# Four chained cross-attentions on one core: second layer through its values in fp32, epsilon on ScalarE, two layer norms centred in the weights, a new order of steps

## The reference, cut to what matters

```python
x = x + softmax(Q K^T / 16) V Wo + bo            # L0: Q from x, K and V from ctx
# L1: two attentions on layer norms, then a layer norm and a dense layer
x1n = ln(x) * g1 + b1 ; x2n = ln(ctx or side) * g2 + b2
x = x + attn_a(x1n, ctx_n) + attn_v(x1n, side_n)
x = x + ln(x) * g + b @ fc_W + fc_b
# L2: softmax over the queries (axis 1), not the keys; then a layer norm
w = softmax((x Wq + bq)(ctx Wk + bk)^T / 16, axis=1)
x = ln(w (ctx Wv + bv) + x) * gamma + beta
x = x + softmax(Q K^T / 16) V Wo + bo            # L3: like L0
```

## Time and profile before

| | value |
|---|---|
| profiled execution | 647.02 us, span 645.1 us |
| median of three runs | 645.7 us |
| TensorE matmul (PE) | 590.6 us busy, 4852 instructions |
| TensorE weight load (PEld) | 569.8 us, 4852 |
| VectorE (DVE) | 558.3 us, 1690 |
| GpSimd (POOL) | 524.4 us, 699 |
| ScalarE (ACT) | 434.4 us, 1462 |
| DMA | 43.97 MB, mean 68 GB/s |
| mean granted TensorE clock | 0.988 |

### The profile page before, as it was taken

One profiled execution on the slowest core, in us unless ns is written; L12 is line 12 of the kernel. 1 busy time (PEld: TensorE's weight loads), 2 busy tenths in 40 slices (PEclk: granted clock), 3 DMA queues, 4 the chain that ended last, 5 costly groups with the idle time before them and its releaser, 6 DMA issues. The chain is left out here.

```text
span 645.1 us, 16889 instructions
## 1 busy us (share of the span) xinstructions
PE 590.6 (92%) x4852; PEld 569.8 (88%) x4852; DVE 558.3 (87%) x1690; ACT 434.4 (67%) x1462; POOL 524.4 (81%) x699
## 2 busy tenths in 40 slices
PE   5987999998789988998998999999999999999976
PEld 4977998898789988988998999898999889999975
DVE  0687799999898989899879898989998998997993
ACT  1568867775658776666767768766668668767543
POOL 5489999997779988888888699888889898876772
PEclk8999999999999999998999999999999999999998
DMA  8931110031121221111212112113022000000011
GB/s 243 359 127 65 52 50 34 26 123 59 50 74 60 74 69 49 59 65 44 86 64 66 43 59 91 58 58 108 10 77 97 27 25 18 1 19 17 18 50 50
DMA packets 29514, 43.97 MB, mean 68 GB/s; under 512 B 2672, under 2 KB 21232, under 8 KB 29424
## 3 DMA queue, kind: packets, MB, share of 16 engines
q1 hardware_dynamic: 29424, 42.89, 20.2%
HBM read 34.49 MB, written 8.39 MB: 66 GB/s over the span
## 5 line engine op out<-in xcount | busy, mean ns | idle before, releaser
L900 ACT ACTIVATE prob_L<-bank,neg_max_L 128x128 f32<-128x128 f32 x320 | 114.4, 374 | 78.8 <-DVE neg_max_L L1168 77.5
L1316 POOL TENSOR_SCALAR xhat_ln<-x,rstd_ln,shift_ln 128x256 f32<-128x256 f32 x128 | 72.2, 573 | 20.4 <-issue 10.1
L1034 DVE TENSOR_TENSOR oT_lo_L<-bank,oT_hi_L 128x256 fp32r<-128x256 f32 (+1 forms) x128 | 60.9, 480 | 18.7 <-ACT oT_hi_L L843 18.0
L1310 POOL TENSOR_TENSOR rstd_ln<-var_eps_ln,minus_half 128x2 f32<-128x2 f32 x64 | 45.5, 711 | 31.5 <-DVE var_eps_ln L1135 28.5
L843 ACT ACTIVATE oT_hi_L<-bank 128x256 fp32r<-128x256 f32 (+1 forms) x128 | 57.1, 451 | 20.0 <-PE bank L666 18.9
L843 ACT ACTIVATE xT_hi_L<-bank 128x512 fp32r<-128x512 f32 (+1 forms) x96 | 58.1, 613 | 17.7 <-PE bank L636 15.9
L900 ACT ACTIVATION_READ_ACCUMULATOR prob_L<-bank,neg_max_L 128x1 f32 x320 | 67.4, 211 | 0.0
L1168 DVE TENSOR_REDUCE neg_max_L<-bank 128x2 f32<-128x256 f32 (+1 forms) x128 | 59.8, 479 | 3.0 <-PE bank L660 2.1
L843 ACT ACTIVATE probT_L<-bank 128x256 f32<-128x256 f32 (+1 forms) x96 | 44.2, 467 | 23.1 <-PE bank L644 23.0
L653 PE MATMUL bank<-xT_hi_L,M_hi_L 128*128 128x256 f32 x128 | 40.5, 316 | 9.6 <-DVE xT_lo_L L1034 5.4
L644 PE MATMUL bank<-ident,prob_L 128*128 128x128 f32 x256 | 44.1, 276 | 5.5 <-ACT prob_L L900 4.2
(11 more groups left out here) (208 smaller groups left out, 2400.3 us busy)
## 6 DMA issues: line engine op xcount, KB each, us to landing
x_in<-in_x SPq DMA_DIRECT2D x32, 512.0 KB, 3.5
ctx_in<-in_ctx SPq DMA_DIRECT2D x32, 256.0 KB, 2.7
out<-y SPq DMA_DIRECT2D x32, 256.0 KB, 2.2
side_in<-in_side SPq DMA_DIRECT2D x32, 128.0 KB, 2.1
WqT_L<-in_L_WqT SPq DMA_DIRECT2D x3, 256.0 KB, 4.0
Wo_L<-in_L_Wo SPq DMA_DIRECT2D x2, 256.0 KB, 4.3
WkT_L<-in_L_WkT SPq DMA_DIRECT2D x3, 128.0 KB, 5.3
WvT_L<-in_L_WvT SPq DMA_DIRECT2D x2, 128.0 KB, 3.6
```

The costliest lines, as they stand in the source:

```text
L900: last = activation(at(prob[k], g)[:, b, :], block(bank, b), ACT.Exp, bias=at(neg_max[k], g)[:, b:b + 1], accum_out=at(total[k], g)[:, b:b ...
L1034: dve.tensor_tensor(to, of, hi.bitcast(F32), ALU.subtract).then_inc(done[step], 1)
L1310: pool.tensor_tensor(at(rstd[k], g)[:], at(var_eps[k], g)[:], minus_half[:, 0:n], ALU.pow).then_inc(done[f"rstd_{k}"], 1)
L1316: last = pool.tensor_scalar(at(to, g)[:, n, :], tile, at(rstd[k], g)[:, n:n + 1], at(shift[k], g)[:, n:n + 1], ALU.mult, ALU.add)
```

## The change

- **Second layer.** O_L2, its sums, oT_hi_L2, oT_lo_L2, sums_L2 and x3_bias go. A new step V_L2 on TensorE multiplies the hi and lo parts of ctx^T by Wv (six fp32r matmuls of 256 columns) and v_L2 on VectorE adds the bias row while it evicts. OUT_L2 then is one plain fp32 product of 256 columns per sample, probabilities times values, and out_L2 adds x3 itself. hi_ctx and lo_ctx also wait until V_L2 has read their buffers.
- **Epsilon.** The four additions per group become activations on ScalarE (Identity with epsilon as bias column), between VectorE's mean and GpSimd's rstd.
- **Centring.** keys and ln1 are no longer shifted: GpSimd multiplies by rstd alone. The mean is taken out of WqT, WkT and WvT of L1a and L1v on VectorE at the start, after gains have been multiplied into them (WqT on VectorE, the others on GpSimd) from broadcast rows; new columns bqp and bvp carry the norm's biases. M0 and N0 of L1 go. M and N of L1 no longer need scale columns.
- **Loads.** Rows for g1, b1, g2 and b2 of both attentions (each 256 wide for L1's x side, 128 wide for the keys) replace the two gains; fewer columns in `cols`. L3's weights use L0's buffers and their loads wait for L0's products M, m, N and n.
- **Order.** All due times in STARTS (now of 94 steps) and PREPARATIONS are new, for example M_L1a from 1027 to 1381, M_L1v from 1116 to 2081, N_lo_L1v from 1478 to 2929, m_col_L3 from 2352 to 3377; V_L2 stands straight behind B2 in most groups. Rings: V2 three buffers, x3_bias and token_sums gone, the others unchanged.

```diff
+            def load_qk_L3():
+                prepared(sp, "M_L0")
+                prepared(sp, "m_L0")
+                two("L3", "WqT", "WkT", "qk")
+
+            def load_vo_L3():
+                prepared(sp, "N_L0")
+                prepared(sp, "n_L0")
+                two("L3", "WvT", "Wo", "vo")
+
...
+            def load_rows_wq(a):
+                def of():
+                    replicated(rows[f"{a}_b1"], f"{a}_b1", f"rows_wq_{a}")
+                    replicated(rows[f"{a}_g1"], f"{a}_g1", f"rows_wq_{a}")
+                return of
+
+            def load_rows_wkv(a):
+                def of():
+                    replicated(rows[f"{a}_g2"], f"{a}_g2", f"rows_wk_{a}")
+                    replicated(rows[f"{a}_b2"], f"{a}_b2", f"rows_wv_{a}")
+                return of
 
...
-            def O_L2(g):
+            def V_L2(g):
+
+                if g == 0:
+                    prepared(pe, "Wv2_lo")
+                pe.wait_ge(done["lo_ctx"], g + 1)
+                bank = bank_for(pe, "V_L2", g)
+                hi, lo = at(ctxT_hi, g), at(ctxT_lo, g)
+                for b in range(GROUP):
+                    to = bank[:, b * D:(b + 1) * D]
+                    mm(to, block(hi, b), Wv2_hi[:], start=True, stop=False)
+                    mm(to, block(hi, b), Wv2_lo[:], start=False, stop=False)
+                    last = mm(to, block(lo, b), Wv2_hi[:], start=False, stop=True)
+                last.then_inc(done["V_L2"], 1)
+
+            def OUT_L2(g):
+                pe.wait_ge(done["v_L2"], g + 1)
                 pe.wait_ge(done["prob_L2"], g + 1)
-                bank = bank_for(pe, "O_L2", g)
-                p = at(prob["L2"], g)
+                bank = bank_for(pe, "OUT_L2", g)
                 for b in range(GROUP):
-                    mm(block(bank, b), at(ctx_in, g)[:, b, :], p[:, b, :], start=True, stop=True)
-                for b in range(GROUP):
-                    last = mm(bank[:, TOK + b:TOK + b + 1], p[:, b, :], ones_col[:], start=True, stop=True)
-                last.then_inc(done["O_L2"], 1)
-
-            def OUT_L2(g):
-                if g == 0:
-                    prepared(pe, "Wv2_lo")
-                pe.wait_ge(done["oT_lo_L2"], g + 1)
-                projected("L2", g, [(Wv2_hi, Wv2_lo)])
+                    last = mm(bank[:, b * D:(b + 1) * D], at(prob["L2"], g)[:, b, :], at(V2, g)[:, b, :], start=True, stop=True)
+                last.then_inc(done["OUT_L2"], 1)
 
...
+            def eps_of(k, eps):
+                def of(g):
+                    if g == 0:
+                        prepared(act, "constants")
+                    act.wait_ge(done[f"mean_{k}"], g + 1)
+                    earlier(act, f"rstd_{k}", g, len(var_eps[k]))
+                    activation(at(var_eps[k], g)[:], at(mean_var[k], g)[:, :, 1], ACT.Identity,
+                               bias=epsilon[eps][:, 0:1]).then_inc(done[f"eps_{k}"], 1)
+                return of
...
-            def sums_L2(g):
-                act.wait_ge(done["O_L2"], g + 1)
-                earlier(act, "x3_bias", g, len(token_sums))
-                copied(at(token_sums, g)[:], bank_of("O_L2", g)[:, TOK:TOK + GROUP], "sums_L2")
-
...
+            def centred(w, sums_of, wait):
+
+                n = w.shape[2]
+                dve.tensor_reduce(sums_of[:], w[:], AX.X, ALU.add, negate=True).then_inc(done["small"], 1)
+                dve.wait_ge(done["small"], wait + 1)
+                dve.tensor_scalar(sums_of[:], sums_of[:], 1.0 / n, None, ALU.mult).then_inc(done["small"], 1)
+                dve.wait_ge(done["small"], wait + 2)
+                for t in range(T):
+                    last = dve.tensor_scalar(w[:, t, :], w[:, t, :], sums_of[:, t:t + 1], None, ALU.add)
+                return last
+
+            small = {}
+
+            def smalls(n):
+
+                small["raised"] = small.get("raised", 0) + n
+                return small["raised"] - n
+
+            def wq_of(a):
+                def of():
+                    w, product_of, b1 = stage[a]["WqT"], product["wq"], sums[f"b1_{a}"]
+                    dve.wait_ge(weights[f"{a}_qk"], TWO)
+                    dve.wait_ge(weights[f"rows_wq_{a}"], TWO)
+                    dve.wait_ge(weights["cols"], ONE)
+                    before = smalls(6)
+                    dve.tensor_tensor(product_of[:], w[:], rows[f"{a}_b1"][:].unsqueeze(1).to_broadcast([P, T, D]), ALU.mult).then_inc(done["small"], 1)
+                    dve.wait_ge(done["small"], before + 1)
+                    dve.tensor_reduce(b1[:], product_of[:], AX.X, ALU.add).then_inc(done["small"], 1)
+                    dve.wait_ge(done["small"], before + 2)
+                    dve.tensor_tensor(b1[:], b1[:], cols[:, COLS.index(f"{a}_bq"), :], ALU.add).then_inc(done["small"], 1)
+                    dve.wait_ge(done["small"], before + 3)
+                    dve.tensor_scalar(bqp[a][:].rearrange("p t o -> p (t o)"), b1[:], SCALE, None, ALU.mult)
+                    dve.tensor_tensor(w[:], w[:], rows[f"{a}_g1"][:].unsqueeze(1).to_broadcast([P, T, D]), ALU.mult).then_inc(done["small"], 1)
+                    dve.wait_ge(done["small"], before + 4)
+                    centred(w, sums[f"wq_{a}"], before + 4).then_inc(done[f"wq_{a}"], 1)
+                return of
+
...
+            def bvp_of(a):
+                def of():
+                    prepared(dve, f"wv_gained_{a}")
+                    dve.wait_ge(weights["cols"], ONE)
+                    before = smalls(1)
+                    b2 = sums[f"b2_{a}"]
+                    dve.tensor_reduce(b2[:], product["wv"][:], AX.X, ALU.add).then_inc(done["small"], 1)
+                    dve.wait_ge(done["small"], before + 1)
+                    dve.tensor_tensor(bvp[a][:].rearrange("p t o -> p (t o)"), b2[:], cols[:, COLS.index(f"{a}_bv"), :],
+                                      ALU.add).then_inc(done[f"bvp_{a}"], 1)
+                return of
+
...
-            def moments(k, g, tiles, eps, mean_used_by):
+            def moments(k, g, tiles):
 
                 st, mv = at(stats[k], g), at(mean_var[k], g)
                 for n, tile in enumerate(tiles):
                     last = dve.bn_stats(st[:, n, :], tile)
                 last.then_inc(done[f"stats_{k}"], 1)
                 dve.wait_ge(done[f"stats_{k}"], g + 1)
-                if mean_used_by:
-                    earlier(dve, mean_used_by, g, len(mean_var[k]))
+                earlier(dve, f"eps_{k}", g, len(mean_var[k]))
                 for n in range(len(tiles)):
                     last = dve.bn_aggr(mv[:, n, :], st[:, n, :])
                 last.then_inc(done[f"mean_{k}"], 1)
-                dve.wait_ge(done[f"mean_{k}"], g + 1)
-                earlier(dve, f"rstd_{k}", g, len(var_eps[k]))
-                if g == 0:
-                    prepared(dve, "constants")
-                dve.tensor_tensor(at(var_eps[k], g)[:], mv[:, :, 1], epsilon[eps][:, 0:len(tiles)], ALU.add).then_inc(done[f"var_{k}"], 1)
 
             def stats_keys(g):
                 dve.wait_ge(at(landed["ctx"], g), times_landed("ctx", g))
                 dve.wait_ge(at(landed["side"], g), times_landed("side", g))
                 tiles = [at(ctx_in, g)[:, b, :] for b in range(GROUP)] + [at(side_in, g)[:, b, :] for b in range(GROUP)]
-                moments("keys", g, tiles, EPS_L1, "shift_keys")
+                moments("keys", g, tiles)
 
...
-            def shift_of(k):
-                def of(g):
-                    dve.wait_ge(done[f"rstd_{k}"], g + 1)
-                    earlier(dve, f"norm_{k}", g, len(shift[k]))
-                    dve.scalar_tensor_tensor(out=at(shift[k], g)[:], in0=at(mean_var[k], g)[:, :, 0], scalar=-1.0,
-                                             in1=at(rstd[k], g)[:], op0=ALU.mult, op1=ALU.mult).then_inc(done[f"shift_{k}"], 1)
-                return of
+                moments("ln2", g, [at(x4, g)[:, b, :] for b in range(GROUP)])
+
+            def shift_ln2(g):
+                dve.wait_ge(done["rstd_ln2"], g + 1)
+                earlier(dve, "norm_ln2", g, len(shift["ln2"]))
+                dve.scalar_tensor_tensor(out=at(shift["ln2"], g)[:], in0=at(mean_var["ln2"], g)[:, :, 0], scalar=-1.0,
+                                         in1=at(rstd["ln2"], g)[:], op0=ALU.mult, op1=ALU.mult).then_inc(done["shift_ln2"], 1)
...
-            def x3_bias_of(g):
+            def v_L2(g):
                 if g == 0:
                     dve.wait_ge(weights["row_L2"], ONE)
+                dve.wait_ge(done["V_L2"], g + 1)
+                earlier(dve, "OUT_L2", g, len(V2))
+                dve.tensor_tensor(at(V2, g)[:], bank_of("V_L2", g)[:].rearrange("p (b d) -> p b d", d=D), every(bias["L2v"]),
+                                  ALU.add).then_inc(done["v_L2"], 1)
+
+            def out_L2(g):
                 dve.wait_ge(done["out_fc"], g + 1)
-                dve.wait_ge(done["sums_L2"], g + 1)
-                for b in range(GROUP):
```

(25 more changed lines are left out.)

260 lines of the change are left out of this document (135 added, 125 removed), and 358 rows, old and new, of tables (COPIES, EMPTIED_BY, PREPARATIONS, STARTS).

## The result

The changed kernel takes 601.2 us (median of 4 runs, 600.2 to 601.7) against 646.0 (644.9 to 648.2) for the kernel before on the same chip: a ratio of 0.930 with a 95% interval of 0.927 to 0.933. The forecast was 610 in a range of 594 to 636. The profiled execution took 600.2 us with a span of 598.1; its mean granted clock was 0.985 (0.988 before).

The account below looks back on a forecast made before the run. VectorE's SBUF-only instructions, held up by GpSimd, were taken to starve PE, which lost 50 us in the middle. 647.0 − 35 (middle) − 6 (ends) + 3.2 (second layer) + 2 (preparations) = 611, median 610 us; range 594 to 622, high end 636.

Parts of the forecast that it names:

- Rival (c): Nothing changes, since PE is full already (449 of 480 us busy): 651 us, or 646 to 649; chance 0.06.
- The −35: Middle, 80 to 560 us: at the 3.4% loss of its best comparable stretches, 430 us of work takes 445 us.
- That is about one for one: In two 50 us stretches, VectorE held up 7.1 and 3.0 us while PE lost 8.3 and 2.8.
- T: Theory on trial: VectorE instructions that stand still while GpSimd works empty TensorE, one for one.
- Epsilon's hold-up: VectorE's epsilon additions, all tensors in SBUF, stand still until GpSimd's running instruction is over: 43.0 us of 76 held up.
- I charge no PE time: Epsilon's 128 activations on ScalarE, 0.18 us each, 23 us (23 to 53), are hidden in its 142 us free.
- Rival (b): ScalarE's queue: eps steps wait for a mean and hold exps; 0.35 us each on PE's path gives 655 us; chance 0.08.
- GpSimd's norms: Norms of keys and ln1 with a constant in place of a shift column: GpSimd saves 0.45 us a group.
- Rival (a): GpSimd is next to bound: if it cannot exceed 86%, −14 us in the middle, 631 us; chance 0.20.
- The fp32 product: OUT_L2 on PE: two products of two instructions, 4 x 0.222 = 0.89 us a group; net +3.2 us with the second layer's trades.
- Preparations: VectorE's centring of L1a and L1v weights at the start: some 14 us, 25 us slack as cover, taken +2 us.
- near 440 to 455: VectorE's busy time in us after the change, from 558 to about 438 plus preparations.

Follow-up runs that it names:

- f: All of the change in the kernel before's order (its due times for shared steps), with eight V2 buffers: 616.5 us, ratio 0.957.
- g: Kernel before with the new second layer alone (V_L2, fp32 OUT_L2, v_L2), old order, eight V2 buffers: 640.0 us, ratio 0.994.
- l: g with epsilon and all shifts on VectorE in 128x1 pieces, old order: 631.2 us, ratio 0.980.
- n: g with epsilon on ScalarE, shifts and norms as before: three executions at 625.2 to 626.2 us, one at 615.7; median 625.6, no ratio formed.
- h: g with epsilon added as a constant and the shifts in 128x1 pieces: 643.5 us, ratio 0.999.
- b: Changed kernel with epsilon back on VectorE as a tensor_scalar with a constant (one SBUF input): 617.3 us, ratio 0.958.
- a: Changed kernel with epsilon's four additions back on VectorE as a tensor_tensor of two SBUF tiles: 618.5 us, ratio 0.960.
- j: a with epsilon on VectorE in single 128x1 columns, ten instructions a group: 612.1 us, ratio 0.950.
- m: Changed kernel with GpSimd's norms of keys and first layer norm adding a column of zeros in place of multiplying by a constant: 607.6 us, ratio 0.942.
- e: Kernel before with epsilon added as a constant by tensor_scalar and the shifts in 128x1 pieces: 643.2 us, ratio 0.997.
- i: Changed kernel with the last shift (second layer's norm) as two 128x1 tensor_scalars: 601.0 us, ratio 0.934.

## Why the prediction was right, and where not

**The outcome.** The direction and the range held; the forecast was 36 us of gain, and 45 came. By the sum's own terms: the middle gave 44 us for 35; the two ends 4.6 (42.9 lost to 38.3, by the earlier trace rows and the table), preparations included, for 6 less 2; the work grew from 552.2 to 554.1 us by the ruler, 1.9 for 3.2 (twelve small matmuls went, and the ruler has the forecast's price of the fp32 product in it). The reading that PE's busy time overstates it and that it lost 50 us carried the forecast, and it held: pace in the middle 8.4 matmuls per us (forecast about 8.5), 7.9 before. Rival (c), that PE was full, fell with it. The −35 was not made with the one-for-one rate: it took the whole middle to the pace of its best stretches. That the total came so near is in part luck. The stretches were picked for their small hold-up, which was one price among several; f, which lacks only the order, gives 36.4 in the middle and loses 3.8 more at the ends, and the order, priced at nothing, brought the rest. The forecast thus lies between two kernels that it did not tell apart: f (616.5 us) would have been 6 above the forecast, after is 9 below it.

**The step that failed** is "That is about one for one", the price of a stalled VectorE microsecond. Two stretches in which hold-up and loss happened to agree were read as a rate. Over eight stretches of 50 us of the kernel before (100 to 300, 350 to 400, 450 to 600) the three lines were held up for 52 us and TensorE lost 38; from 500 to 550 it was 8.7 for 4.5. The runs show this in its place, in the middle and in the old order:

| kernel | hold-up | VectorE busy | TensorE loses |
|---|---|---|---|
| before | 62 | 439 | 50 |
| g | 49 | 417 | 40 |
| l | 0 | 419 | 32 |
| n | 30 | 395 | 27 |
| f | 6 | 379 | 14 |

Where the hold-up went and nothing took its place on VectorE (before, g, n, f), 57 us less of it came with 36 less of loss, 0.6 to one; work left VectorE with it, and from n to f GpSimd's norms got lighter too, so even that is no rate of hold-up alone. Where short instructions took its place (g to l), 49 us less of it gave 8. g, h and l fell short of what T forecast for them. In the new order epsilon's long stalls, in place of short instructions of the same total, cost 5 to 6 us (b or a against j). And between f and after VectorE's busy time is the same, while the kernel's time differs by 15 us.

What gave the 45 us instead, as far as the runs part it: along the old order, 4 for the second layer (before to g), then 13 in the middle for epsilon's leaving (g to n), 13.5 there for centring and its lighter norms less 6 at the start (n to f; rough, since n's total is), and **15 for the new order** (f to after, up to 5 of them the clock's). Taken from the other end, epsilon back costs 17 (5 to 6 for its long stalls, 11 for the same time in short instructions) and GpSimd's heavier norms 6.5. These don't add up to one sum, and should not: each was taken away from a different rest, and a, b, j and m run in an order that was made for the kernel after, so that their costs include some misfit.

**Step by step.**
- *Epsilon's hold-up*: the mechanism is right, the condition was too narrow. I had "all its tensors in SBUF", which b confirms with one input, and rested it on "two SBUF inputs ... contend ..., one does not". Additions of a constant on 128x2 and 128x4 are held up to 1.4 and 2.3 us (b), up to 4.0 in e; of the 128x1 forms (with pointers to columns), all in SBUF too, none passes 217 ns, so "all its tensors in SBUF" was also too wide. And the wait is not for one GpSimd instruction alone: the one of 4.0 us spans three whole ones. The Trainium skill (SBUF — State Buffer, "Who interferes with whom") also says that tensor_scalar contends in its 2-port mode, when its operands meet the conditions; my sentence had left that half out. With that half the runs with 128x2 and 128x4 agree; that single columns escape is what the runs show, and that section doesn't say it.
- *"I charge no PE time" for ScalarE's epsilon*: held as far as the runs show, although the activation takes 0.30 us, not 0.18 (39.6 us in all, within the 23 to 53). Rival (b), due at 0.28 us each on PE's path, did not come: in the middle ScalarE is still idle for 101 us, and the waits behind the steps are shorter than those that vanished (14.9 us for the mean, 59 less for neg_max).
- *GpSimd's norms*: 0.372 and 0.479 us, 0.46 a group, as forecast; but they were given no time of their own in the sum, and m shows 6.5 us. Rival (a) had the right engine and the wrong limit: GpSimd went to 88% (421 of 480), not above 90, and what it was relieved of counted.
- *The fp32 product*: four instructions in 0.86 us, for 0.89. The Trainium skill's four passes (FP8 and Floating Point Precision, "TensorE Precision Notes") gave 0.94; the trace is 9% under it.
- *Preparations*: mis-sized at 14 us, their pieces in VectorE's timeline add up to some 17. L1090's first product takes 1.75 us beside GpSimd, and VectorE is busy 29 us of the first 40, where it was 18. M_lo of L1a comes at 22.1 us (17.8 before), the first x-hat at 45.4 (43.1), and they are most of the chain from 11.5 to 32 us. The cover of 25 us was no cover: 2.3 us of delay show at the first x-hat, about the 2 charged.
- *VectorE*: 470 us, forecast 438 plus preparations, "near 440 to 455". The preparations explain 17 us of the 32 above 438. The rest is the way of counting: neighbouring instructions overlap, so that before's lines add up to 619 us where VectorE is busy for 558, and a line that is taken off whole takes too much. The lines' sum fell by 101 us, the busy time by 88. "No line but the third shift past 0.8 us" was wrong for the preparations alone.
- *"The new order and buffers ... have no price of their own"*: wrong. f shows 15 us (up to 5 of them the clock's), with epsilon's leaving the largest part, though the same sentence had said that the order's waits "decide how much of the middle is filled".

**What stays open.** How centring and epsilon share their gain in the old order, n being spread by its clock; why epsilon's short instructions cost 11 us on VectorE, and whether by their time or by their place (the neg_max wait of j points to steps that stand in front of the reductions, but no run moved them); what hold-up and work on VectorE cost each by itself (h has less hold-up than g, as much VectorE time in the middle, and loses 7.5 us more there); and what an order made anew for a, j or m would give back. None of the runs beat the kernel after: i equals it.
